# A five-stage transformer kernel on one core: two banks for the attention's sums and two for its other products, variances on VectorE, and output products of the state-space stage at other steps

## What is computed

```
x = x + 0.5 * moe_ffn(layernorm(x))       # 8 experts, top 2, hidden 512, gelu
x = x +       ssm(layernorm(x))           # 32 heads, state 64, R = 2, chunks of 128, rotary, gated rms
x = x + 0.5 * moe_ffn(layernorm(x))
x = x + 0.5 * lora_moe(layernorm(x))      # base product + 8 experts of rank 16, top 2
x = x +       attention(layernorm(x))
x = x + 0.5 * lora_moe(layernorm(x))
```

```
# ssm: per chunk of 128 tokens and head
y_intra = (C B^T * decay, causal) @ X ;  y_inter = C @ state ;  state = decay * state + B^T @ X
y = rms((y_intra + y_inter) * silu(z)) @ W_out
# attention: 16 heads of 8 features
q, k = l2norm(heads(x Wq)), l2norm(heads(x Wk))
p = softmax(where(causal, q k^T * scale, -10000) / 1.5)
out = ((p @ v) @ Wo + bo) * 0.5
# layernorm: m = mean(x), v = mean((x - m)^2), (x - m) / sqrt(v + eps)
```

## Time and profile before

| | |
|---|---|
| median of 3 runs | 1444.87 us (1443.93 to 1449.31) |
| the profiled execution | 1445.81 us |
| span of its trace | 1444.1 us |
| PE busy | 1166.5 us, 81% of the span |
| DVE busy | 1036.0 us, 72% |
| ACT busy | 804.3 us, 56% |
| POOL busy | 760.8 us, 53% |
| mean granted TensorE clock | 0.856 |

### The profile page before, as it was taken

One profiled execution on the slowest core, in us unless ns is written; L12 is line 12 of the kernel. 1 busy time (PEld: TensorE's weight loads), 2 busy tenths in 40 slices (PEclk: granted clock), 3 DMA queues, 4 the chain that ended last, 5 costly groups with the idle time before them and its releaser, 6 DMA issues. The chain is left out here.

```text
span 1444.1 us, 32988 instructions
## 1 busy us (share of the span) xinstructions
PE 1166.5 (81%) x11380; PEld 739.8 (51%) x11380; DVE 1036.0 (72%) x2301; ACT 804.3 (56%) x1477; POOL 760.8 (53%) x1115
## 2 busy tenths in 40 slices
PE   7679963698988989889757996358998998898894
PEld 6369952455545545555636995343443444343332
DVE  6959973888888897899786997574756766673433
ACT  3768854445235325411346885026777677787881
POOL 2366633763674675355346664557547565544421
PEclk6779986698889989999658998557999999999997
DMA  8025340000000000000412333000000010000000
GB/s 280 18 88 178 90 60 22 22 9 2 23 9 2 19 13 1 2 2 2 138 61 68 90 90 54 20 15 16 9 15 12 5 31 10 7 8 9 1 16 8
DMA packets 55714, 55.09 MB, mean 38 GB/s; under 512 B 9882, under 2 KB 44484, under 8 KB 55556
## 3 DMA queue, kind: packets, MB, share of 16 engines
q1 hardware_dynamic: 46468, 34.37, 7.6%
q0 software_dynamic: 9088, 18.63, 5.8%
HBM read 32.26 MB, written 20.71 MB: 37 GB/s over the span
## 5 line engine op out<-in xcount | busy, mean ns | idle before, releaser
L2146 ACT ACTIVATE l_probs<-l_ps 128x1024 f32<-128x1024 f32 (+1 forms) x320 | 287.8, 947 | 100.4 <-PE l_ps L2032 99.8
L784 POOL DMA_INDIRECT ffn_yg<-y_rows,ffn_index x156 | 156.3, 1002 | 82.6 <-PE ffn_ps_t L799 39.4
L2051 PE MATMUL l_ps<-l_probs,l_vs 128*32 128x512 f32 (+3 forms) x1536 | 165.6, 520 | 30.2 <-POOL l_probs L2228 22.7
L2228 POOL TENSOR_SCALAR_AFFINE_SELECT l_probs<-l_probs 128x256 f32<-128x256 f32 x256 | 110.1, 449 | 140.5 <-ACT l_probs L2146 139.5
L867 ACT ACTIVATE ffn_hT<-ffn_ps_h,experts_b1T,experts_scales 128x256 f32<-128x256 f32 x312 | 151.1, 563 | 30.7 <-PE ffn_ps_h L814 29.4
L266 POOL DMA_INDIRECT combine_og<-o_rows,combine_place x128 | 139.9, 1093 | 51.4 <-issue 27.6
L1310 PE MATMUL ssm_ps<-ssm_X,ssm_near 32*32 32x256 f32 x2048 | 138.3, 422 | 1.9 <-DVE ssm_Y L1753 1.9
L2032 PE MATMUL l_ps<-l_qkT 32*128 32x512 f16 (+3 forms) x768 | 109.3, 339 | 16.0 <-ACT l_probs L2146 13.9
L1552 POOL TENSOR_TENSOR ssm_u_out<-ssm_ysum,ssm_zx 128x256 f32<-128x256 f32 x32 | 69.0, 2156 | 99.8 <-DVE ssm_ysum L1764 99.7
L892 DVE SCALAR_TENSOR_TENSOR ffn_h<-ffn_hT,experts_scales,ffn_h 128x512 f16<-128x512 f32 x156 | 117.2, 752 | 5.5
L830 PE MATMUL ffn_ps_o<-experts_w,ffn_h 128*128 x624 | 113.1, 220 | 2.2 <-DVE ffn_h L892 2.0
(11 more groups left out here) (354 smaller groups left out, 2865.6 us busy)
## 6 DMA issues: line engine op xcount, KB each, us to landing
o_rows<-ffn_out_sb SPq DMA_DIRECT2D x78, 128.0 KB, 2.1
y_rows<-ffn_y SPq DMA_DIRECT2D x8, 512.0 KB, 5.1
kept_w<-experts_w SPq DMA_DIRECT2D x16, 256.0 KB
experts_w<-kept_w SPq DMA_DIRECT2D x16, 256.0 KB, 5.9
ffn_yg<-y_rows,ffn_index POOLq DMA_INDIRECT x156
x_res<-in_L_attn_x SPq DMA_DIRECT2D x4, 512.0 KB, 6.1
prep_raw<-in_L_ffn_W SPq DMA_DIRECT2D x1, 2048.0 KB, 10.4
prep_raw<-in_L_ffn_W SPq DMA_DIRECT2D x8, 256.0 KB, 5.6
```

What stands on the lines that cost most here:

```text
L784: g_.indirect_dma_start(yg[:, i % RING, j].rearrange("p n d -> p (n d)"), None, w.y_rows.ap(), bass.IndirectOffsetOnAxis(ap=index[:, n:n + ...
L2051: ins = t_.matmul(ps_o[VP * h:VP * h + VP, q0 % H:q0 % H + width], vs[:, s % 2, kb, h, :], probs[:, n % PSLOTS, i, at:at + width], start=( ...
L2146: s_.activation(probs[:, w % PSLOTS, i:i + n, 0:width], ps_s[w % 2][:, i:i + n, 0:width], ACT.Exp, scale=SCALE / (UNIT * UNIT)).then_inc(S ...
L2228: g_.affine_select(p, p, [[0, n], [1, P]], ALU.is_ge, 0.0, base=0, channel_multiplier=-1).then_inc(S["m_done"], 1)
```

## The change

In the state-space stage PE's `project_out` goes from step 21 to 22.6 and DVE's `finish` from 23.5 to 25; the input projections of groups 2 to 7 start 2 steps earlier with gathers and statistics, while their transposes and products keep their place (`TURN`); the read of the product "vn" is planned later; and `LATER` moves `dots`, `near_levels` and `far_levels` of a tile behind its transposes where the planner has moved these by more than 1.5 steps (tiles 6, 14 and 22). In the last stage `ps_o` gets two banks, used by turns, and the ring keeps two; the wait for the copy of the sums is for the step before last. POOL's `norm` keeps the power alone; the rest is DVE's `spread`, seven operations in three rounds, right behind the statistics. In the state-space part the lines of the changed file have numbers 3 higher.

```diff
+        TURN = [NORM + (2 if g >= 2 else 0) for g in range(GROUPS)]
-        G_AT = [C_AT[g // 2] - (46 if g % 2 else 68 if g else 55.9) for g in range(GROUPS)]
+        G_AT = [C_AT[g // 2] - (46 if g % 2 else 68 if g else 55.9) - (TURN[g] - NORM) for g in range(GROUPS)]
...
-            streams["g", g] = G_AT[g], [(("g", g, "y"), NORM + 6, NORM + 8)] + [(("g", g, j), NORM + 10 + 1.5 * j, NORM + 12 + 1.5 * j) for j in range(GROUP)]
+            streams["g", g] = G_AT[g], [(("g", g, "y"), TURN[g] + 6, TURN[g] + 8)] + [(("g", g, j), TURN[g] + 10 + 1.5 * j, TURN[g] + 12 + 1.5 * j) for j in range(GROUP)]
...
-            streams["c", b] = ... (("c", b, "vn"), 13.2, 18.6), ...
+            streams["c", b] = ... (("c", b, "vn"), 13.2, 21), ...
...
-            streams["r", n] = K[n], [(("r", n), 21, 23.5)]
+            streams["r", n] = K[n], [(("r", n), 22.6, 25)]
...
+        LATER = [max(0, uses.at(("t", n), -16) - (K[n] - 16) - 1.5) for n in range(TILES)]
...
                 def dots(n):
-                    yield -14
+                    yield -14 + LATER[n]
...
-                            yield -13
+                            yield -13 + LATER[n]
...
                 def project_out(n):
-                    yield 21
+                    yield 22.6
...
                 def far_levels(n):
-                    yield -10.8
+                    yield -10.8 + LATER[n]
...
                 def near_levels(n):
-                    yield -12
+                    yield -12 + LATER[n]
...
                 def finish(n):
-                    yield 23.5, ("r", n)
+                    yield 25, ("r", n)
...
-        bank = ctx.enter_context(nc.psum_tensor(f"{tag}_ps", [P, 5, 512], F32))
-        bank2 = ctx.enter_context(nc.psum_tensor(f"{tag}_ps2", [P, 3, 512], F32))
+        bank = ctx.enter_context(nc.psum_tensor(f"{tag}_ps", [P, 6, 512], F32))
+        bank2 = ctx.enter_context(nc.psum_tensor(f"{tag}_ps2", [P, 2, 512], F32))
         ps_s = [bank[:, 0:2, :], bank[:, 2:4, :]]
-        ps_o = bank[:, 4, :]
+        ps_o = [bank[:, 4, :], bank[:, 5, :]]
...
-        uses = Uses([bank2[:, i, :] for i in range(3)], ...
+        uses = Uses([bank2[:, i, :] for i in range(2)], ...
...
-                                if s:
-                                    pe.wait_ge(S["oT_read"], s)
+                                if s >= 2:
+                                    pe.wait_ge(S["oT_read"], s - 1)
...
             def _(pool):
                 def norm(i, g):
-                    yield 0
...
+                    yield 2
                     ts = group(g)
...
+                    pool.wait_ge(S[f"spread{i}"], g + 1)
+                    g_.tensor_tensor(core.rstd[:, ts], core.tmp2[:, ts], core.minus_half[:, 0:GROUP], ALU.pow).then_inc(S[f"rstd{i}"], 1)
...
+                    dve.wait_ge(S[f"counted{i}"], g + 1)
+                    spread(i, g)
+
+                def spread(i, g):
...
+                    v.tensor_tensor(half, even, odd, ALU.subtract).then_inc(chain.sem, 1)
+                    v.tensor_tensor(mean, even, odd, ALU.add).then_inc(chain.sem, 1)
+                    v.tensor_tensor(var, core.stats[:, ts, 2], core.stats[:, ts, 5], ALU.add).then_inc(chain.sem, 1)
+                    chain.n += 3
+                    dve.wait_ge(chain.sem, chain.n)
+                    v.tensor_tensor(half, half, half, ALU.mult).then_inc(chain.sem, 1)
+                    v.tensor_scalar(mean, mean, 0.5, None, ALU.mult).then_inc(chain.sem, 1)
+                    v.tensor_scalar(var, var, 1.0 / D, LN_EPS, ALU.mult, ALU.add).then_inc(chain.sem, 1)
+                    chain.n += 3
+                    dve.wait_ge(chain.sem, chain.n)
+                    chain.link(v.scalar_tensor_tensor(var, half, 0.25, var, ALU.mult, ALU.add))
+                    dve.sem_inc(S[f"spread{i}"], 1)
...
                 def take_experts(g):
...
+                    yield 2.8
+                    dve.wait_ge(combine.counted, (g + 1) * GROUP)
+                    spread(0, g)
...
-                        v.tensor_copy(oTs[:], ps_o).then_inc(S["oT_read"], 1)
+                        v.tensor_copy(oTs[:], ps_o[s % 2]).then_inc(S["oT_read"], 1)
```

More of the change, by code:

```diff
@@ L1207, in project @@
                 def project(g):
-                    yield NORM + 6
+                    yield TURN[g] + 6
                     pe.wait_ge(S["y_ready"], g + 1)
@@ L1214, in project @@
                     for j in range(GROUP):
-                        yield NORM + 10 + 1.5 * j
+                        yield TURN[g] + 10 + 1.5 * j
                         uses.wait_read(pe, ("g", g, "y"))
@@ L1379, in project @@
                     ins.then_inc(S["y_ready"], 1)
-                    yield NORM + 8, ("g", g, "y")
+                    yield TURN[g] + 8, ("g", g, "y")
                     ps = uses.wait(act, ("g", g, "y"))
@@ L1385, in project @@
                     for j in range(GROUP):
-                        yield NORM + 12 + 1.5 * j, ("g", g, j)
+                        yield TURN[g] + 12 + 1.5 * j, ("g", g, j)
                         ps = uses.wait(act, ("g", g, j))
@@ L1390, in project @@
                         uses.read(s_.copy(raw[:, h * GROUP + j, :], ps[:, 0:RAW]), ("g", g, j))
-                    yield NORM + 19
+                    yield TURN[g] + 19
                     for j in range(GROUP):
@@ L1588, in project @@
                         dve.sem_inc(S["spread"], 1)
-                    yield NORM + 22.5
+                    yield TURN[g] + 22.5
                     dve.wait_ge(S["squared"], g + 1)
@@ L1959, in layer1 @@
             streams["e", g] = E_AT[g], [(("e", g, "o"), 1, 3), (("e", g, "out"), 5, 7)]
-        uses = Uses([bank2[:, i, :] for i in range(3)], [sem(f"full{i}") for i in range(3)], [sem(f"free{i}") for i in range(3)], streams)
+        uses = Uses([bank2[:, i, :] for i in range(2)], [sem(f"full{i}") for i in range(2)], [sem(f"free{i}") for i in range(2)], streams)
         with nc.Block(no_gpsimd_drain=True) as block:
@@ L2261, in count @@
                     ins.then_inc(S[f"counted{i}"], 1)
+                    dve.wait_ge(S[f"counted{i}"], g + 1)
+                    spread(i, g)
+                def spread(i, g):
+                    ts = group(g)
+                    even, odd = core.stats[:, ts, 1], core.stats[:, ts, 4]
+                    half, var, mean = core.tmp1[:, ts], core.tmp2[:, ts], core.mean[:, ts]
+                    v.tensor_tensor(half, even, odd, ALU.subtract).then_inc(chain.sem, 1)
[10 more added lines that the diff above has]
+                    dve.sem_inc(S[f"spread{i}"], 1)
                 def lora(i, g):
```

26 lines of the change are left out of this document (3 added, 23 removed).

## The result

The changed kernel takes 1434.24 us (median of 7 runs, 1428.38 to 1442.00) beside 1444.87 (7 runs, 1443.93 to 1449.31); the ratio is 0.9908, interval 0.9889 to 0.9927. That is 10.6 us by the medians and 13.3 by the ratio, where 30 were forecast. The profiled execution of the changed kernel took 1442.00 (span 1439.9) and is the slowest of the seven, so stretches are compared here and not the spans.

A forecast was written before the change was run, and what follows sets the result against it. PE and VectorE, waiting by turns, bound the state-space stage, PE the attention loop. Terms -8, -10, -2.5, -17, -5, +10, +1 sum to -31.5: 1445.8 to 1414.3, median run 1413.4, stated 1415; 8-in-10 range 1394 to 1443.

The forecast's parts named there:

- State-space, VectorE order (-8): State-space stage: `finish` behind `near` and the first state step lets L1734 start before POOL's L1542; -8 us, ends 0 and -13.
- 9.5 stalls: State-space stage: L1734's excess of 13.3 us over 24 executions, counted as some 9.5 stalls of 1.4 us.
- State-space, PE order and gathers (-10): State-space stage: later output product and earlier gathers cut PE's waits for `uT` and `y`, 24.5 us; -10, ends 0 and -24.
- first rival: State-space stage: the orders gain nothing, as DVE's total work is the same; 1433 us, chance 0.20.
- Start and end (-2.5): Attention's start and end: normalizations on VectorE in three rounds save 0.7 us each; -2.5 us, ends 0 and -4.
- Masks and sums (-17): Attention loop: PE waits less for POOL's masks (22.7 us) and the copy of the sums (7.5); -17, ends -6 and -30.
- Two banks (+10): Attention: all other products share two banks, and 17 more tight places wait for ACT reads; +10 us, ends 0 and 34.
- VectorE's new work (+1): Attention: 35 us of added VectorE operations are covered, but stand ahead of copies PE waits for; +1 us.
- The clock behind long waits (-5): Attention loop: shorter waits spare a quarter of some 20 us lost to the low clock; -5 us, ends 0 and -12.
- second rival: Attention: banks at their upper end (1439) or a loop clock of 0.88 (1446) eat the gain; 1443 us, chance 0.12.

The follow-up runs named there:

- ssm_only: State-space edits alone, last stage as in the kernel before: 1437.34 us beside 1448.91, ratio 0.9921.
- ssm_again: State-space edits alone once more, last stage as in the kernel before: 1432.83 us beside 1447.22, ratio 0.9899.
- after_third: The whole change a third time, against the kernel before on the same chip: 1431.67 us beside 1447.22, ratio 0.9894.
- out_only: State-space edits without the earlier gathers (TURN), against the kernel before on a slow chip: 1477.23 us beside 1490.73, ratio 0.9916.
- finish_only: Only VectorE's `finish` moved to step 25, against the kernel before on a slow chip: 1483.75 us beside 1490.73, ratio 0.9955.

## Why the forecast was right in direction and wrong in size

**State-space, VectorE order (-8): right.** The tail is 8.1 us shorter, tiles 8.76 apart (forecast 8.9), and `finish` alone gives 5 to 7 us of time. The count behind it was not: I spread 9.5 stalls over the stage, and only the six of the tail went. In the mixed tiles L1737 meets POOL's product more than before (16.4 us for 12.5), and its mean is 840 ns, not near 550.

**State-space, PE order and gathers (-10): the step that failed first.** I priced the wait for `uT` that goes and did not ask what stands next: the scores need ACT's copy of the transposes, which had been ready because PE stood waiting for `uT` just before. 15.3 us went and 17.0 came, and `y` stayed at 6.2 us where I had said below 3. PE's idle time in the mixed part says what is left of the 10 us: 40.0 and 40.1 in the two traces of before, 38.5, 38.4, 38.5 and 35.2 in those of ssm_only, ssm_again, after and after_third, so 2 to 5 us. The stretch itself was 337.9, 341.2, 341.2 and 331.3 us long in these four, and the low clock, estimated as above, makes most of that spread: 36.9, 40.5, 40.5 and 33.5, where before has 36.3 twice. The runs give the state-space edits 11 and 14 us, of which the tail is 8. On a slow chip PE's order took 6.5 us off by the runs (out_only and finish_only), with less low clock and not less idle time; no trace tells why. My first rival (the orders gain nothing) is excluded.

**Start and end (-2.5): right.** From the last expert's activation to the first exponential the profile before has 93.4 us and after 92.7, where I had 2 us less; from the last exponential to the end 31.9 and 30.8. Together that is 1.8 us. The seven operations take 0.86 us together, 903.94 to 904.80, less than the 1.3 I counted:

```profile
903.94 0.17 DVE L2253 TENSOR_TENSOR ln_tmp<-ln_stats 128x4 f32<-128x4 f32 x1
...
904.64 0.16 DVE L2263 SCALAR_TENSOR_TENSOR ln_tmp<-ln_tmp 128x4 f32<-128x4 f32 x1
```

**Masks and sums (-17): undersized.** 24.4 us went.

**Two banks (+10): undersized.** Idle time fell by 6.5 in all, so 18 us came elsewhere; the rows by line above show some 14 of it ahead of L1977, L2065 and L2018, products that take banks and the transposes of the sums (2.7 + 6.0 + 6.7 where 0.8 + 0.0 + 0.4 stood). And the price is none of the bank alone: 16 or 1 us, by where the variances are made. I had costed the edits of one queue as a sum of terms, and they don't add: of PE's idle time the variances alone took 2.2 us, the banks alone added 6.6, and both together took 6.5.

**VectorE's new work (+1): small.** PE's waits for VectorE's `y` in the loop rose from 1.9 to 3.9 us, and how much of that is the new work and how much the banks was not tested.

**The clock behind long waits (-5): the term with the wrong sign, +5.5 in the loop.** I reasoned from the place behind the 4.65 us wait and wrote that the loop "fell only behind waits of 2 us and more". My trace did not say so. Behind a wait of 1.34 us that ended at 1113.15 the clock stood at 1.00, which is the first row below; behind another of 1.34, that ends at 1323.70, it fell to 0.50, the 1.2 GHz level of the two:

```profile
1113.30:1119.70 6.40, 3.55 (x38) 1.24 (x31) 1.67 (x6) 4.83 (x6) 5.51 (x17) 1.00 0.03 8
1324.60:1327.80 3.20, 3.20 (x20) 1.32 (x20) 1.59 (x4) 1.50 (x2) 2.30 (x6) 0.50 0.00 0
```

```profile
1323.70 1.25 PE L2051 MATMUL l_ps<-l_probs,l_vs 128*32 128x512 f32 x8 [1.34 <-POOL l_probs L2228]
```

After, it is 0.50 from behind a wait of 1.76 on, with one of 1.25 inside the stretch, and again behind one of 1.26:

```profile
1107.44 0.64 PE L2054 MATMUL l_ps<-l_probs,l_vs 128*32 128x256 f32 x8 [1.76 <-POOL l_probs L2212]
...
1110.47 1.94 PE L2054 MATMUL l_ps<-l_probs,l_vs 128*32 128x512 f32 x8 [1.25 <-ACT l_probs L2149]
...
1145.84 0.79 PE L2065 MATMUL l_ps<-ident,l_oTs 128*128 128x128 f32 x4 [1.26 <-DVE l_zwT L2317]
```

```profile
1108.80:1118.90 10.10, 8.85 (x45) 3.61 (x45) 4.89 (x15) 4.35 (x7) 4.15 (x10) 0.50 0.04 9
1146.30:1153.00 6.70, 6.70 (x32) 2.50 (x30) 5.89 (x20) 2.89 (x3) 4.40 (x6) 0.50 0.12 29
```

So shorter waits did not spare the low clock: it costs 24.6 us in place of 19.2.

The Trainium skill (TensorE: Matmul & The Clock Gate, A second HAM failure mode) speaks of kernels that cycle banks with short idles between; my text named it and gave it too little. It fits the three traces of these loops from usual chips. The two from slow chips, with the same idle time and 14.5 and 15.9 us of low clock, say that the waits alone do not decide it; what does was not found. The Trainium skill (TensorE: Matmul & The Clock Gate, Part 1: The HAM clock gate) says that one kernel's slow matmuls at its start differ in number from run to run; no run here was made to test that.

So the forecast's second rival (the banks and the clock eat it) describes the last stage, and not the total. In the loop -24.4 (masks and sums) + 17.9 (other idle time) + 5.5 (low clock) + 2.4 (other busy time) = +1.4, where -11 was forecast. What the total gained is the tail's, and in other executions than this slowest one the mixed part's, 331.3 us in after_third.

## What to carry to other kernels

When an instruction is moved out of the way of a wait, look for the next one in its queue and ask what it needs: the old wait may have been its cover. Edits that feed one queue (who makes the variances, how many banks, when the masks come) have to be tried in all combinations, since here each alone lost and together they did not. And a saved wait counts only with the clock. Take PE's busy time in the stretches at 0.50 beside its idle time, and see that the stretches compared hold the same number of matmuls: here busy time alone rose by 7.9 us, of which the clock was 5.5.
